# Projections stage: four key-part buffers, and the query casts moved ahead of a context block and a row tile

## The reference

```python
attn_out = jnp.where(vm, ctx @ v_dense, ctx @ l_dense)
hidden_states = residual + attn_out
ci = rms_norm(hidden_states, ln_post_cross_w)
cq = heads(ci @ cq_w, NH, CHD)
ckv = encoder_outputs @ ckv_w
ck, cv = jnp.split(ckv, 2, axis=-1)
```

## Time and profile before

| | |
|---|---|
| median of 3 runs | 2267.29 us |
| profiled execution | 2259.36 us |
| its span | 2257.2 us |
| TensorE busy | 2042.4 us (90%) |
| VectorE busy | 1409.7 us (62%) |
| ScalarE busy | 990.9 us (44%) |
| GpSimd busy | 473.5 us (21%) |
| DMA, mean | 105 GB/s |

### The profile page before, as it was taken

The page is one execution under the profiler, slowest core; times in us unless marked ns, Lnnn a source line. Parts: engine busy times, 40 slices in busy tenths (PEclk is TensorE's granted clock), DMA queues, the critical chain, the costliest instruction groups (busy, mean ns, idle before and its releaser), DMA issues. The chain is left out here.

```text
span 2257.2 us, 32387 instructions
## 1 busy us (share of the span) xinstructions
PE 2042.4 (90%) x12597; PEld 1334.1 (59%) x12614; DVE 1409.7 (62%) x1952; ACT 990.9 (44%) x1724; POOL 473.5 (21%) x483
## 2 busy tenths in 40 slices
PE   7999997999989995788579999999998899999788
PEld 5667765777755553577424444444434677878666
DVE  4324436666457775555489999999952576666344
ACT  1312215444325552444318888888884222221111
POOL 0221131233201112222001122122132212212111
PEclk9999997999979997899859999999999999999989
DMA  4112202332476634655552543543501333334242
GB/s 159 72 67 96 71 1 94 118 112 104 145 169 161 160 86 140 218 208 209 155 100 49 95 80 76 94 87 72 101 17 46 105 95 103 104 105 114 61 105 66
DMA packets 176918, 238.12 MB, mean 105 GB/s; under 512 B 26166, under 2 KB 105146, under 8 KB 174550
## 3 DMA queue, kind: packets, MB, share of 16 engines
q1 hardware_dynamic: 168600, 224.76, 37.0%
q0 software_dynamic: 7856, 10.90, 1.8%
q10 hardware_dynamic: 288, 0.08, 0.0%
HBM read 169.61 MB, written 63.96 MB: 103 GB/s over the span
## 5 line engine op out<-in xcount | busy, mean ns | idle before, releaser
L1984 DVE TENSOR_REDUCE quarters<-ps 128x2 f32<-128x804 f32 x512 | 483.1, 991 | 52.1 <-PE ps L2018 50.6
L1949 ACT ACTIVATE pT_x<-ps 128x512 f32<-128x512 f32 (+1 forms) x832 | 451.6, 595 | 103.1 <-PE ps L2046 75.6
L2018 PE MATMUL ps<-kx_ring,qx_ring 63*128 63x402 f32 x1024 | 234.3, 470 | 38.4 <-DMA kx_ring<-cross_k_by_part 26.6
L2061 PE MATMUL ps<-pT_x,vx_ring 128*17 128x256 f32 (+1 forms) x3328 | 261.0, 387 | 0.2 <-ACT osb_x L1931 0.2
L2018 PEld LDWEIGHTS ps<-kx_ring,qx_ring 63*128 63x128 f32 x1024 | 100.4, 193 | 231.6 <-DVE quarters L1984 123.9
L106 PE MATMUL ps<-mi_h,w_hi 128*128 128x512 f32 (+1 forms) x440 | 174.4, 396 | 33.4 <-DVE w_lo L102 23.7
L2046 PE MATMUL ps<-qx_ring,kx_ring 64*128 64x512 f32 (+1 forms) x832 | 174.7, 416 | 6.4 <-ACT pT_x L1949 2.6
L108 PE MATMUL ps<-mi_l,w_hi 128*128 128x512 f32 (+1 forms) x440 | 173.7, 395 | 0.0
L107 PE MATMUL ps<-mi_h,w_lo 128*128 128x512 f32 (+1 forms) x440 | 173.2, 394 | 0.0
L2202 POOL TENSOR_TENSOR sg<-sg,keep_all 128x512 f32<-128x512 f32 (+1 forms) x55 | 87.5, 1590 | 408.4 <-ACT sg L2181 408.4
L1216 DVE TENSOR_REDUCE row_max_s<-ps 128x1 f32<-128x384 f32 (+3 forms) x176 | 109.4, 633 | 67.9 <-PE ps L1248 67.1
(11 more groups left out here) (315 smaller groups left out, 4313.5 us busy)
## 6 DMA issues: line engine op xcount, KB each, us to landing
kx_ring<-cross_k_by_part SPq DMA_DIRECT2D x96, 200.2 KB, 7.3
qkv_l<-self_q_by_part SPq DMA_DIRECT2D x48, 256.0 KB, 4.2
qkv_h<-self_k_by_part SPq DMA_DIRECT2D x48, 256.0 KB, 6.6
w_raw<-L_xattn_l_gate SPq DMA_DIRECT2D x40, 256.0 KB, 2.9
w_raw<-L_xattn_l_up SPq DMA_DIRECT2D x40, 256.0 KB, 2.9
w_raw<-L_xattn_l_down SPq DMA_DIRECT2D x40, 256.0 KB, 2.7
cross_v_by_group<-v_aug SPq DMA_DIRECT2D x16, 442.0 KB, 4.0
vx_ring<-cross_v_by_group SPq DMA_DIRECT2D x16, 442.0 KB, 10.3
```

The lines of the kernel that those rows point to most:

```text
L1949: nc.scalar.activation(pT[0:kn, u % 3, j, :], ps[0:kn, 5 + v % 3, :], ACT.Exp, scale=SCALE)\
L1984: nc.vector.tensor_reduce(out=quarters[:, g % 2, pair, :, q, quarter], in_=ps[:, at:at + 2, 0:MAXW], axis=AX.X, op=ALU.max)\
L2018: last = nc.tensor.matmul(ps[:, at + par, 0:MAXW], q_r[rows, g % RING, pair, q * P:(q + 1) * P], k_r[rows, g % RING, pair, k0:k0 + MAXW], ...
L2061: last = nc.tensor.matmul(ps[j * HD:j * HD + CHD + 1, 4, queries], v_r[0:kn, g % RING, kt, j, :], pT[0:kn, u % 3, j, queries], start=kt == ...
```

## The change

Two things in `projections`, nothing outside it.

The key parts get four buffers each: kc_h and kc_l have `KEEP` = 4 slots, with four store semaphores in place of two. A unit waits for the stores of unit j - 4.

The casts (ScalarE) and rests (VectorE) of the two query banks are moved up, ahead of the next batch's context block 1 and row tile 3.

```diff
-            wl, s_uk = [s[f"s_wl{i}"] for i in range(RAW)], [s["s_uk0"], s["s_uk1"]]
-            NW, NB, RING = len(tiles), len(KEY_BANKS), 4
+            wl, s_uk = [s[f"s_wl{i}"] for i in range(RAW)], [s[f"s_uk{i}"] for i in range(4)]
+            NW, NB, RING, KEEP = len(tiles), len(KEY_BANKS), 4, 4
...
-                kh, kl = sb("kc_h", [P, 2, S], f32r, ctx=ctx), sb("kc_l", [P, 2, S], f32r, ctx=ctx)
+                kh, kl = sb("kc_h", [P, KEEP, S], f32r, ctx=ctx), sb("kc_l", [P, KEEP, S], f32r, ctx=ctx)
...
-                            if j >= 2:
-                                act.wait_ge(s_uk[j % 2], 32 * (j // 2))
-                            nc.scalar.activation(kh[:, j % 2, 0:wide], ps[:, bank["k", b, m], 0:wide], ACT.Copy).then_inc(s["s_kh"], 1)
+                            if j >= KEEP:
+                                act.wait_ge(s_uk[j % KEEP], 32 * (j // KEEP))
+                            nc.scalar.activation(kh[:, j % KEEP, 0:wide], ps[:, bank["k", b, m], 0:wide], ACT.Copy).then_inc(s["s_kh"], 1)
...
-                            round_context(NB * b + 5)
-                            if b + 1 < B:
-                                round_rows(NW * (b + 1) + 3)
                             for c in range(ET):
                                 act.wait_ge(s["s_q"], ET * b + c + 1)
                                 if b:
                                     act.wait_ge(s["s_uq"], 32 * ET * b)
                                 nc.scalar.activation(qh[:, c, :], ps[:, Q_BANKS[c], :], ACT.Copy).then_inc(s["s_qh"], 1)
+                            round_context(NB * b + 5)
+                            if b + 1 < B:
+                                round_rows(NW * (b + 1) + 3)
...
-                            rest_context(NB * b + 5)
-                            if b + 1 < B:
-                                mask_rows(NW * (b + 1) + 3)
                             for c in range(ET):
                                 dve.wait_ge(s["s_qh"], ET * b + c + 1)
                                 nc.vector.tensor_tensor(out=ql[:, c, :], in0=ps[:, Q_BANKS[c], :], in1=qh[:, c, :].bitcast(f32),
                                                         op=ALU.subtract).then_inc(s["s_ql"], 1)
+                            rest_context(NB * b + 5)
+                            if b + 1 < B:
+                                mask_rows(NW * (b + 1) + 3)
```

More of the change, by code:

```diff
@@ L1320, in projections @@
             names = ("s_fl s_wl0 s_wl1 s_wl2 s_wl3 s_wh s_ws s_att s_hin s_own s_high s_low s_wd s_add s_c s_ch s_cl s_v s_vc s_k s_kh "
-                     "s_kl s_sq s_sum s_tot s_rt s_n s_nhi s_nlo s_q s_qh s_ql s_ms s_uh s_uv s_uk0 s_uk1 s_uq s_scl")
+                     "s_kl s_sq s_sum s_tot s_rt s_n s_nhi s_nlo s_q s_qh s_ql s_ms s_uh s_uv s_uk0 s_uk1 s_uk2 s_uk3 s_uq s_scl")
             ctx, sems = stage(names)
             s = dict(zip(names.split(), sems))
-            wl, s_uk = [s[f"s_wl{i}"] for i in range(RAW)], [s["s_uk0"], s["s_uk1"]]
-            NW, NB, RING = len(tiles), len(KEY_BANKS), 4
+            wl, s_uk = [s[f"s_wl{i}"] for i in range(RAW)], [s[f"s_uk{i}"] for i in range(4)]
+            NW, NB, RING, KEEP = len(tiles), len(KEY_BANKS), 4, 4
             NT = NW + 2 * ET
@@ L1427, in _ @@
                                         sp.dma_start(k_heads_d[b, part, c * P:(c + 1) * P, k0:k0 + wide],
-                                                     src[:, j % 2, 0:wide].bitcast(f32)).then_inc(s_uk[j % 2], 16)
+                                                     src[:, j % KEEP, 0:wide].bitcast(f32)).then_inc(s_uk[j % KEEP], 16)
                             sp.wait_ge(s["s_vc"], KT * (b + 1))
@@ L1439, in _ @@
                         sp.wait_ge(s["s_uq"], 32 * ET * B)
-                        for m in range(2):
-                            sp.wait_ge(s_uk[m], 32 * ET * NB * B // 2)
+                        for m in range(KEEP):
+                            sp.wait_ge(s_uk[m], 32 * ET * NB * B // KEEP)
                     @block.gpsimd
@@ L1605, in rest_keys @@
                                 dve.wait_ge(s["s_kh"], j + 1)
-                                nc.vector.tensor_tensor(out=kl[:, j % 2, 0:wide], in0=ps[:, bank["k", b, ET * kb + c], 0:wide],
-                                                        in1=kh[:, j % 2, 0:wide].bitcast(f32), op=ALU.subtract)\
+                                nc.vector.tensor_tensor(out=kl[:, j % KEEP, 0:wide], in0=ps[:, bank["k", b, ET * kb + c], 0:wide],
+                                                        in1=kh[:, j % KEEP, 0:wide].bitcast(f32), op=ALU.subtract)\
                                     .then_inc(s["s_kl"], 1)
```

## The result

The changed kernel takes 2243.6 us (median of 6 runs, 2237.74 to 2246.84), the kernel before on the same chips 2263.65 us (6 runs, 2260.84 to 2267.91). The ratio is 0.9906, 95% interval [0.9888, 0.9924]. The ratios here are of means; 20 us is the difference of the medians, 21 us that of the means. The profiled execution took 2237.74 us, its span is 2235.6 us, 21.6 us shorter than the span before.

What follows compares the result with a forecast made beforehand. TensorE's waits in the projections stage, about 49 of 234 us, were taken to bound it; gains of 6.6 + 5.6 + 5.6 + 1.45 = 19.3 us less 2.9 for the clock gave 16.4 us, a median of 2251 us, range 2244 to 2260.

Steps and rivals of the forecast that it cites:

- The buffers: Projections, key parts: kc_h's store wait becomes a context-load wait, queries end early, and four buffers alone give nearly nothing.
- The stop before the dense product: TensorE, between queries and first dense tile: a new stop released by att_l, 3.8 us, some 3.3 in batch 1.
- The landing of the context block: Next batch's context load lands 9.6 and 9.3 us after issue in batches 0 and 1, about 0.4 us before chx.
- the rival of the early stores: Key-part stores delay the context load by 2.55 us in each of three batches; gain 8.7 us, 2258.6; chance 0.15.
- The query casts first: At the batch changes: qc_h follows the third att_h, so TensorE resumes dense work 6.6, 5.6 and 5.6 us sooner.
- The fourth row tile and the scaling at nothing: Work moved behind the query casts costs nothing: fourth row tile has 1.4 us of cover, VectorE before the add about 3.
- The clock: TensorE's dense product: 1.45 us gained from batch 0's old fall, 2.9 us lost to two falls after new stops.
- the prediction's bound of three falls: Upper bound of the clock charge: TensorE's clock falls after all three new stops before dense tiles, costing 4.4 us.
- The sign by which it was read: First matmul after a TensorE stop taking 0.50 us, not 0.80, was taken to show the clock had not fallen.
- The sum: Projections stage: 6.6 + 5.6 + 5.6 + 1.45 = 19.3 us, less 2.9 for the clock, gives 16.4 us.
- The range: Whole kernel: 2244 (full 20.3 us gain, 3 us scatter) to 2260 us (early-stores rival, 1.5 us).

Runs made afterwards that it cites:

- the first edit alone: Four key-part buffers instead of two, with the old order of query casts and rests, against the kernel before: ratio 1.0002 [0.9990, 1.0014].
- the control: The kernel before run again with no edit, against the kernel before: ratio 0.9990 [0.9975, 1.0005].
- the filled kernel before: The kernel before plus twelve 512-column matmuls, results unread, in TensorE's stop by qc_l, against the kernel before: ratio 1.0000 [0.9987, 1.0012].

## Why the prediction was right and wrong, step by step

- *The buffers.* Right. The wait for a store became a wait for the context block, the queries end early, and the first edit alone gives nothing (1.0002). The stop before the dense product was put at 3.8 and 3.3 us; it was 4.36, 3.43 and 4.28.
- *The landing of the context block.* Right, and the rival of the early stores is out: with four stores issued behind it while it was under way (from 925.59 to 929.06 in batch 0) the block landed 9.8, 9.4 and 9.5 us after issue in the three batches, against 9.6, 9.3 and 9.9 before. All 16 loads of the changed kernel:

```profile
DMA to landing us min/median/max: 2.0/3.8/9.8
```

- *The query casts first.* Right in place, too large by some 2 us. Put at 36.0, 33.3 and 33.8 us after the add, the seventh dense matmul came at 37.2, 33.3 and 35.4. Part of the lateness is the clock: the first six dense matmuls took 2.0 and 2.7 us in the late batches instead of 1.5. The rest, 0.7 and 0.4 us, is att_l, which releases the first of them that much later. Against the means of four and three profiles the fronts are 4.9, 5.1 and 3.8 us shorter: 13.8 us, where the terms said 6.6 + 5.6 + 5.6 = 17.8. Of these 4.0 us, 2.0 are the slow first six matmuls, in the mean of the three profiles (the prediction had charged such falls to the clock), and 1.2 are the first profile's front, 121.0 us against a mean of 119.8.
- *The fourth row tile and the scaling at nothing.* Right: no stop stands before the fourth dense tile in the changed kernel, and VectorE still waits 2.18 to 3.72 us for the last dense matmul before the add. Such a stop appears, with 0.99 us at most, once the stream is loaded later.
- *The clock.* This is the step that failed. "The same work took 16.92 us in batch 0 and 15.47 us in batch 1" gave 1.45 us for all that the clock cost in the kernel before, from one profile, while the three stops of the new kernel were charged with 2.9 us; so the clock was to take 1.45 us from the gain. Four profiles show tails that are 1.5, 9.0, 9.0 and 4.7 us above 3 x 15.47, 6.05 us on average. The three of the changed kernel have 1.1, 3.0 and 2.5 us, 2.2 on average, and lose another 2.0 us in the first six matmuls, which take 1.5 us per batch at the full clock. So the clock cost about 6 us before and 4.2 us now, and it gives 1.8 us where it was to take 1.45. The charge for the new stops was too small as well (4.2 us is nearly the prediction's bound of three falls, 4.4), but the cost before, 6.05 us put at 1.45, was off by most.
- *The sign by which it was read.* The prediction took a first matmul of 0.50 us behind a stop as a sign that the clock had not fallen. In its own profile the reading comes out right, but the sign does not carry: in the control the seventh matmul took 0.50 us in the first and third changes of batch, and the tails were 17.05 and 18.64 us. The level of the whole tail has to be read.
- *The sum.* By the means of the profiles it is 13.8 us of front, 3.85 of tail and 0.6 at the end of the stage (36.1 us from the last add before, 35.5 now), together 18.2 us where the terms gave 16.35. The errors partly cancel: 4.0 us too much in the front, 5.3 too little in the tail, 0.6 not counted at the end. That the total came this close is in part luck.
- *The range.* It ended at the full 20.3 us, and 3 us for scatter, below a median of 2267.29. That median came from 3 runs; with 3 more it is 2263.65. Of the error of the time, 7.4 us, half is the gain (3.65 us) and half this (3.6 us).
- *What stays open.* The last 4 us of the gain have no cause that timed runs prove. The profiles put them into the clock of the dense tiles; the filled kernel before, which has that clock up in its profile, was not faster in its timed runs.

## What to carry to other kernels

When a wait is removed, look up when the next operand on the same engine lands: here it had landed only 0.4 us before ScalarE took it, so the wait changed its name and the four buffers gave nothing. They were worth 15 to 20 us once that load was issued a block earlier. Move what a stopped engine waits for ahead of prefetches for work that comes later; that reordering alone gave the whole gain. What a stop costs in clock varies between executions of the same kernel by several us, so it is read from several profiles or kept as a wide bound.

## What the hardware showed that I had not expected

The clock behind a stop of TensorE is not given by the program, nor by the length of the stop alone. In the kernel before, at the second change of batch, the tail took 19.7 us after stops of 3.04 and 3.00 us, with a granted clock of 0.77 and 0.76 over it, and 15.5 us after stops of 3.26 and 3.25 us, with 1.00. At the first change of batch the clock also fell after a stop of only 2.35 us (next matmul 0.79 us, tail 17.0 us). The earlier stop by kc_l differed too, 3.40 and 3.43 us before the long tails, 3.26 and 3.25 before the short; no run separates the two. And in a stage with unchanged code an execution gains or loses 4 to 5 us near 400 us; two profiles side by side show it as if the change had done it.
